# Extra matrix products placed ahead of six waits of TensorE in a vision block kernel

## What is computed

```python
h = tok(x)                        # 1x1 conv to 16, batch norm, relu, 1x1 conv to 9 filters per pixel,
                                  # then each pixel's own 3x3 filter over its neighbours: (4, 4096, 64)
h = h + attn(layernorm(h))        # softmax(Q K^T / 8) V, one head of width 64, 4096 tokens per image
h = h + ffn(layernorm(h))         # router picks one of 32 experts per token; relu(relu(y W1 + b1) W2 + b2)
```

## Time and profile before

| what | value |
|---|---|
| median of 3 runs | 1134.55 us (1134.44 to 1134.91) |
| the profiled execution | 1132.9 us |
| its span, first to last instruction | 1131.0 us |
| TensorE matmul busy in the span | 1097.7 us (97%) |
| TensorE's granted clock, mean over the span | 0.984 of full speed |
| ScalarE busy, VectorE busy | 628.4 us, 491.2 us |

### The profile page before, as it was taken

The page is one execution under the profiler, slowest core; times in us unless marked ns, Lnnn a source line. Parts: engine busy times, 40 slices in busy tenths (PEclk is TensorE's granted clock), DMA queues, the critical chain, the costliest instruction groups (busy, mean ns, idle before and its releaser), DMA issues.

```text
span 1131.0 us, 29094 instructions
## 1 busy us (share of the span) xinstructions
PE 1097.7 (97%) x12634; PEld 555.7 (49%) x12634; DVE 491.2 (43%) x1101; ACT 628.4 (56%) x698; POOL 10.5 (1%) x35
## 2 busy tenths in 40 slices
PE   6699999999999999999999999999999999999996
PEld 1233344555544555555555555555555555555542
DVE  6788766437072552626346181633413040301323
ACT  2356656556566465655646555564655556465551
POOL 3000000000000000000000000000000000000000
PEclk9799999999999999999999999999999999999997
DMA  5645612113005120212104021040000000000000
GB/s 152 144 116 123 150 42 57 39 39 76 2 14 132 39 67 11 57 42 67 39 12 97 13 64 30 11 95 11 11 3 11 2 11 1 11 2 10 2 2 20
DMA packets 15346, 51.62 MB, mean 46 GB/s; under 512 B 2846, under 2 KB 6046, under 8 KB 14828
## 3 DMA queue, kind: packets, MB, share of 16 engines
q1 hardware_dynamic: 15212, 49.68, 19.1%
HBM read 41.77 MB, written 4.75 MB: 41 GB/s over the span
## 4 chain that ended last, share of the span: by engine, by line
PE 94%; DVE 2%; DMA 1%; ACT 1%; issue 1%; DVEq 0%; SPq 0%; ACTq 0%
PE z_ps L671 39%; PE scores L660 38%; PE both L627 4%; PE both L642 4%; PE both L519 2%; PE both L623 1%; DMA filter_ring<-filters 1%; PE both L650 1%; PE both L567 1%; PE both L557 1%; PE both L607 1%; PE both L588 1%; PE both L598 1%; PE both L634 0%; PE scores L547 0%
## 5 line engine op out<-in xcount | busy, mean ns | idle before, releaser
L881 ACT ACTIVATE probs<-scores 128x1024 f32<-128x1024 f32 x504 | 488.6, 1021 | 427.0 <-PE scores L660 427.0
L660 PE MATMUL scores<-g_t,keys_t 64*64 64x512 f32 x4096 | 516.0, 594 | 1.9 <-ACT g_t L860 1.2
L671 PE MATMUL z_ps<-probs,keys 64*64 64x512 f32 x4096 | 512.8, 590 | 0.0
L660 PEld LDWEIGHTS scores<-g_t,keys_t 64*64 64x64 f32 x4096 | 219.7, 134 | 228.6 <-issue 222.3
L671 PEld LDWEIGHTS z_ps<-probs,keys 64*64 64x64 f32 x4096 | 205.0, 133 | 183.2 <-issue 178.9
L1148 DVE COPY o_sb<-both 128x512 f32<-128x512 f32 x14 | 9.7, 691 | 319.8 <-PE both L642 319.8
L1048 DVE TENSOR_TENSOR hres<-hres,tap_product 128x504 f32<-128x504 f32 (+1 forms) x128 | 89.1, 696 | 11.2 <-issue 0.9
L1043 DVE SCALAR_TENSOR_TENSOR tap_product<-filter_ring,w,xin 128x504 f32<-128x504 f32 (+1 forms) x120 | 89.0, 742 | 8.0 <-DMA filter_ring<-filters 4.6
L627 PE MATMUL both<-y_t,w 64*64 64x512 f32 x464 | 64.3, 597 | 0.0
L873 ACT ACTIVATE hidden<-both 128x1024 f32<-128x1024 f32 (+1 forms) x58 | 58.5, 1008 | 6.5 <-PE both L627 6.5
L642 PE MATMUL both<-hidden,w 64*64 64x512 f32 x448 | 56.9, 592 | 0.0
(11 more groups left out here) (137 smaller groups left out, 565.6 us busy)
## 6 DMA issues: line engine op xcount, KB each, us to landing
filter_ring<-filters SPq DMA_DIRECT2D x90, 384.0 KB, 5.2
out_dram<-out_sb SPq DMA_DIRECT2D x32, 128.0 KB, 2.4
xin<-x_dram SPq DMA_DIRECT2D x6, 528.0 KB, 9.0
g_t<-g_t SPq DMA_DIRECT2D x24, 128.0 KB, 4.8
hidden<-once_dram SPq DMA_DIRECT2D x1, 930.0 KB, 13.3
hidden<-once_dram SPq DMA_DIRECT2D x1, 576.0 KB, 5.3
filters<-filters_sb SPq DMA_DIRECT2D x30, 18.0 KB
xin<-x_dram SPq DMA_DIRECT2D x1, 384.0 KB, 6.3
```

What stands on the lines that cost most here:

```text
L660: last = T.matmul(scores[rows_of(h), c, r * 512:(r + 1) * 512], keys_t[rows_of(r), i // NQ % 2, k * 128 + 64 * h:k * 128 + 64 * h + 64], g ...
L671: last = T.matmul(z_ps[rows_of(c), h, :], keys[rows_of(h), i // NQ % 2, 2 * k + r, :], probs[rows_of(h), (2 * g + c) % RING, r * 512:(r + ...
L881: A.activation(probs[:, unit % RING, :], scores[:, c, :], ACT.Exp, scale=first_scale[:, 0:1] if n == 0 and g <= ASKED else SCALE).then_inc ...
```

## The change

A helper `stay_at_work` issues, `times` over, the four products of one `score` call with weights and columns that are already there, into PSUM that nobody reads. `fill` calls it ahead of six fills. For the fills of block 15 it stands ahead of `wait_free` and writes into the first half of `scores`; for `xt@1` it stands behind `wait_free` and writes into `both`. In both cases it stands ahead of the fill's own waits. The counts are 7 for `xt@1`, and for block 15: `yt` 2, `lg` 2, `ot` 5, `hid0` 2, `fin` 4.

```diff
+KEPT_AT_WORK = {"xt@1": 7} | {f"{name}@{BLOCKS - 1}": k for name, k in
+                              (("yt", 2), ("lg", 2), ("ot", 5), ("hid0", 2), ("fin", 4))}
...
+            def stay_at_work(banks, times):
+                for _ in range(times):
+                    for r in range(2):
+                        for h in range(2):
+                            T.matmul(banks[rows_of(h), r, :], keys_t[rows_of(r), 0, 64 * h:64 * h + 64],
+                                     g_t[rows_of(r), 0, r, :], start=True, stop=True)
...
                 if name.startswith(NONE):
                     return
+                if i == BLOCKS - 1:
+
+                    stay_at_work(scores[:, 0, :].rearrange("p (r n) -> p r n", r=2), KEPT_AT_WORK.get(full, 0))
                 wait_free(full)
+                if i != BLOCKS - 1:
+                    stay_at_work(both, KEPT_AT_WORK.get(full, 0))
                 k = places.of[full]
```

## The result

The changed kernel has a median of 1140.83 us over five runs (1138.85 to 1142.42), the kernel before 1134.44; the ratio is 1.0058, with an interval of 1.0037 to 1.0078. It is slower, as forecast, but by 6.4 us (4.2 to 8.8) instead of 3.8, and outside the range of 1135.4 to 1140.2. The profiled execution took 1141.74 us.

What follows compares the result with a forecast made beforehand. TensorE was taken as the bound from 60.00 to 1094.90 us, then a chain between TensorE, ScalarE and VectorE. Opening +0.99 and end +2.78 made +3.8 on 1132.9, 1136.7; with 1.65 carried, 1138.3 us (ratio 1.0033), range 1135.4 to 1140.2.

Steps and rivals of the forecast that it cites:

- the price of a repetition: At all six places: one repetition, the four products of a `score` call, takes 0.86 us at the upper clock.
- Rival B: All six places: repetitions take half as long, the holes swallow them, and the kernel is faster, 1130.4 us; chance 0.07.
- places 2 to 6: Fills `yt`, `lg`, `ot`, `hid0`, `fin` of block 15: repetitions overshoot, the clock gives some back, net +2.78 us.
- the clock in the hidden layer: From `hid0@15` to `o2@15`: the clock stays at its upper level, giving back 2.75 us.
- the term of `fin@15`: Ahead of `fin@15`: four repetitions make it 1.64 us late, with no clock won.
- place 1: Ahead of `xt@1` in the opening: seven repetitions lose 2.69 us, the clock gives back 1.70, net +0.99 us.
- rival D: Ahead of `xt@1`: the branch is no longer hidden, repetitions start late, up to +3.1 us, 1138.3 to 1141.4; chance 0.08.
- the 1.65 us: Whole kernel: the runs' median exceeds the profiled execution by 1.65 us, place unknown, carried whole into the forecast.
- rival C: Opening and block 15: the runs' extra 1.65 us is half-clock time the change wins back, 1136.7 us; chance 0.14.

Runs made afterwards that it cites:

- e2: Changed kernel with the seven repetitions for `xt@1` alone, none at the five places in block 15: 1137.10 us, ratio 1.0028.
- e3: Changed kernel with the seven repetitions for `xt@1` issued ahead of the flag and branch of block 0: 1138.87 us, ratio 1.0044.
- e4: Changed kernel with TensorE's unusual side of block 0's branch cut to one wait, leaving out image 0's shifted softmax: 1136.09 us, ratio 1.0019.
- e12: The cut branch of e4 with its seven repetitions for `xt@1`, and the end counts of e5: 1130.04 us, ratio 0.9961.
- e1: Changed kernel without repetitions for `xt@1`, the five places in block 15 keeping their counts: 1138.29 us, ratio 1.0035.
- e11: Changed kernel without the four repetitions ahead of `fin@15`, nothing else changed: 1140.18 us, ratio 1.0043.
- e5: Changed kernel without repetitions for `xt@1`, and in block 15 `yt` 0, `lg` 1, `ot` 3, `hid0` 1, `fin` 0: 1132.12 us, ratio 0.9977.
- e7: Kernel with no repetitions anywhere and the cut branch of e4, against the kernel before: 1134.37 us, ratio 0.9992.
- e10: Changed kernel with the end counts of e5, block 0's flag and branch one group earlier, two repetitions for `xt@1`: 1136.22 us, ratio 1.0012.
- e8: Changed kernel with SyncE's filter loads of block 2 held until block 1's layer norm is written: 1141.93 us, ratio 1.0065.

## Why the prediction was right and wrong

**Right: the price of a repetition.** 56 records take 6.2 us at the upper clock (e2, e3, e4, e12), 0.86 us a repetition with the tail taken off. Rival B falls.

**Right: places 2 to 6 and the clock in the hidden layer.** Worked out +2.78; the profiles of the changed kernel and of e1 have 2.7 and 2.9 more in the rest, e11 confirms the term of `fin@15` (1.6) and e5 that the same places win 2.7 when nothing overshoots.

**Wrong: place 1, in the step "The array is free at about 50.89 + 1.72 = 52.61. Seven repetitions take 6.01 us and end at 58.62".** The array was free at 52.11 in the changed kernel, but the first repetition came 3.80 us later, and then the clock was low for part of them, so that they held the array for 7.73 us instead of 6.01, 1.72 more. The two make the 5.5 us by which the opening missed its sum in that execution. It was rival D, with a chance of 0.08, and the sum had no term for it. My argument against D was that block 4's branch leaves no gap. That row was true and the comparison false: TensorE's code for the unusual side holds, for block 0, a second pass over the whole block (lines 751 to 758), for block 4 only `find_max`, and it is the length of the jump that counts (e4: 4.56 to 0.36 us). The prediction could have been better on this with what it had, by reading the source of the branch and looking for its record in the trace.

The Trainium skill ("Runtime: NRT & Kernel Launch", section "Instruction fetch mechanics") says that a taken branch whose target is not in the fetched window forces a fetch before execution can go on. The trace agrees: 4.56 us against 0.35, and every long branch ends 1.35 to 1.55 us behind the end of a 16 KB fetch. I had cited it and let the row of block 4 overrule it.

D's bound was too small as well. I had capped its price at 3.1 us, the idle time of the kernel before, and let the filler keep the clock up behind it; the hole alone cost 3.8 in the profiled execution, and the clock's fall 1.7 on top. The median, 1140.83, lies inside D's 1138.3 to 1141.4 only because the next error went the other way.

**Wrong in the other direction: the hole was taken from one execution, and the 1.65 us were carried.** The keys were done at 55.69 in the profiled execution of the kernel before. In the 13 other profiles they were done between 56.31 and 57.59 eleven times, and earlier (53.85, 54.59) twice. The hole before `xt@1`, 3.3 us in that execution (52.61 to 55.93), is 5.6 to 6.4 us in those of e1, e5 and e7, which have no repetition there either, so that seven repetitions of 6.0 us were not nearly as long for it as 2.69 us of overshoot say; e4 has 0.3. The 1.65 us between that execution and the median look like this too: e7's profiled execution, at 1134.58, has an opening 1.8 us later and the same rest. Of these 1.8 us, 1.6 are the later `xt@1` (57.51 against 55.93) and 0.2 the stretch from there to `into_z` (5.87 against 5.67), so in it rival C, which took them for time at half clock, had the place right and the kind wrong; in e1 and e5 that stretch is 7.0 us, and the low clock has a share. In e4 it is 3.98 us: against e7 the filler gives back 1.9 us and delays `xt@1` by nothing (57.44 against 57.51). Without the slow branch, place 1 is not +1.0 but some −2.1 (e4 against e1, 1136.09 and 1138.29; e12 against e5, 1130.04 and 1132.12).

**The account.** End: +2.8 worked out, +3.7 (2.7 to 5.2) measured (e1). Opening: +1.0 worked out; measured +2.5 with the branch (e2 against the kernel before; the changed kernel against e1) and −2.1 without. The branch in the open thus costs some 4.6 us in the median, and the change as made loses 6.4. The direction was partly luck: without the slow branch e4 came to 1136.09, +1.5, below the 1136.8 from which the prediction calls the kernel slower. In the opening two errors of opposite sign, −3.1 and +4.6, left 1.5; the other 1.1 us by which the whole misses lies in the end, whose interval in e1 holds the 2.8.

Still open: why the fetch under the branch begins 0.9 to 3.4 us behind its start (the kernel's own transfers sort the profiles, which does not show that they are the cause), the second hole of e10, and a way to have the whole of e12's gain without leaving the unusual side out.

## What to carry to other kernels

Before filling a wait, find out everything that ends it: the profile names only the last releaser, and a slow branch that ends 0.2 us before the data is invisible until work is put behind it. Size a filler from the hole in several executions and from the engine's own rate (here 0.86 us a repetition), and keep it shorter than the hole, since it takes in-order time from the real work: five repetitions in the right places won 2.7 us at the end where fifteen lost as much. Read a row of the clock beside the records' own durations: the changed kernel's row has a 9 over a burst that the records show at the lower level.

## What the runs showed of the hardware that was not expected

- A taken branch of TensorE's sequencer over a long stretch of code took 3.34 to 6.22 us in eleven profiles, over a short one 0.22 to 0.42 us. The long ones ended 1.35 to 1.55 us behind the end of a 16 KB fetch of instructions, in all eleven.
- The sequencer reached that branch about 1.7 us before the array was free (50.90 against 52.61; 50.41 against 52.11; e3: 55.50 against 57.20), and in e3 that was all of it that work ahead of it hid.
- Dense products did not keep the clock up where they came late: behind 3.6 and 3.7 us without work (changed, e11) it was at its lower level while part of them ran, behind 2.0 us (e2, e8) it stayed at the upper one.
